# A cleared scratch tile between any two row gathers of a graph network kernel

## The chip, the cores and the metric

The kernel runs on one core of a Trainium2 chip. The metric is the device time of one execution in microseconds (us), the median of several runs. A core has TensorE (PE in the profile), VectorE (DVE), ScalarE (ACT), GpSimd (POOL) and SyncE (SP), each with a program of its own; they signal each other through semaphores. Sixteen DMA engines move data. An indirect DMA, which takes a list of row numbers, is issued by GpSimd, which is busy for a while with each.

## The reference, cut to what matters

Four graph layers run one after the other on 3125 nodes with 64 features and 50,000 edges. Each begins with a layer norm and a ReLU and adds its result to x. Three of them pass messages along edges:

```
# layer 0
msg  = relu(h[src] + edge_attr_16 @ We + be)
aggr = segment_sum(msg, dst)                  # then a two-layer MLP
# layer 2, three times
hx = h @ W_node[l]
a  = sigmoid(relu(concat(hx[dst], hx[src], edge_attr_3) @ Wa1 + ba1) @ Wa2 + ba2)
out = segment_sum(a * (hx[src] + ef), dst)    # ef: a small MLP of edge_attr_3
# layer 3
h = silu(bn(concat(x_i, x_j - x_i) @ W.T));  x_out = segment_sum(h, row)
```

Layer 1 is ten steps of a normalized propagation. It is done with dense blocks of the adjacency matrix, which are built during layer 0's pass, kept in HBM and streamed in; no row is gathered there.

## The kernel before, in words

The edges are first ordered by destination block and written to HBM by 400 scatters of GpSimd (line 755), as 416 tiles of 128 edges. Four tiles are a unit and eight units a body, so a message pass is 104 units in 13 bodies. There are five passes: one for layer 0, three for layer 2 and one for layer 3. The first is peeled, loops over the middle and peels the end on TensorE, VectorE and ScalarE; on SyncE and GpSimd all 13 bodies are one loop.

In a pass a unit goes through these hands:

- SyncE loads the edges' payload (`pay`, line 632) in four chunks of a body, two units each. It waits until those two units of the body before have been summed (`slots_free`).
- GpSimd (line 770) waits for the chunk, and then issues one gather per tile: eight per chunk, 32 per body, 416 per pass, 2080 in all. A gather brings 128 rows of the node table into `rows`, which has places for eight units. Its landing counts up `gathered[u]`.
- VectorE makes one-hot matrices of the destinations (lines 1102 and 1103), later adds the gathered rows to what TensorE worked out (lines 1115 to 1121), and in layer 0 it also makes the operands of the dense blocks (lines 1079, 1085 and 1087).
- ScalarE evicts and applies the activations: line 1466 (hidden layer) and 1468 in layer 2, 1489 and 1495 in layer 3.
- TensorE turns one-hots and payload (lines 1728 and 1605), multiplies (its matmuls all carry line 1502), and sums the messages of the unit before last into PSUM. The last matmul of that sum counts up `slots_free`.

The loop structure fixes the order on every engine; nothing is scheduled. GpSimd can be up to eight units ahead of the sum. Between passes 1 and 2, beside layer 1, GpSimd also issues 400 scatters of the second edge table (line 728); ahead of every eighth of them stand three small copies on GpSimd (lines 721, 719 and 724), the last of which the next scatters wait for.

`hold` (line 498) is a wait on a semaphore with an increment of a counter `held` that nobody waits for.

Of the kernel before, what the change touches and what calls it, by code (L numbers as in the profile page):

```python
# [34 lines left out]
K = 4  # L35
# [4 lines left out]
BODY = K * U  # L40
# [52 lines left out]
def gnn_kernel(nc, x, src, dst, edge_attr_16, edge_attr_3, edge_weight,  # L93
# [3 lines left out]
    with ExitStack() as ctx:  # L97
        def sb(name, shape, dt=F32):
            return ctx.enter_context(nc.sbuf_tensor(name, shape, dt))

        def sem(name):
            return ctx.enter_context(nc.semaphore(name))
# [20 lines left out]
        g_of = sb("g_of", [128, 1])  # L123
        ones_b = sb("ones_b", [128, EJ], BF16)
        zeros = sb("zeros", [128, CW])
        zeros_b = sb("zeros_b", [128, 512], BF16)
        acc_at = sb("acc_at", [1, 2, T], I32)
        tab_at = sb("tab_at", [1, 2, T], I32)
# [305 lines left out]
        hs_ready = sem("hs_ready")  # L434
        out_done = sem("out_done")
        held = sem("held")

        starts_ready = sem("starts_ready")
        starts_summed = sem("starts_summed")
# [56 lines left out]
        def hold(eng, semaphore, value):  # L496

            eng.wait_ge(semaphore, value)
            eng.sem_inc(held, 1)

        def load_values(eng, at_, lowest, highest):

            _, values = nc.values_load_multi_w_load_instructions(
                at_, engines=(eng.engine,), min_val=lowest, max_val=highest, skip_runtime_bounds_check_because=
                "the tables are worked out from counts of edges, and every entry is within its bounds by construction")
            return values
# [3 lines left out]
        def load_counts(eng, at_, lowest, highest):  # L510
            _, values = nc.values_load_multi_w_load_instructions(at_, engines=(eng.engine,), min_val=lowest, max_val=highest)
            return values
# [168 lines left out]
        def _(pool):  # L681
# [66 lines left out]
            def scatter_dst():  # L748

                for q in range(2 * G2):  # L750
                    h, j0 = q % 2, q * SG
                    pool.wait_ge(staged, q + 1)
                    pool.wait_ge(placed, next(c for c in range(NC_) if j0 + SG <= GR * (CHUNK_AT[c] + CHUNKS[c])) + 1)
                    for j in range(SG):
                        nc.gpsimd.indirect_dma_start(  # L755
                            rows_dst, bass.IndirectOffsetOnAxis(ap=pos_dst[:, j0 + j:j0 + j + 1], axis=0),
                            stage[:, h, j, :], None).then_inc(scattered[h], 16)

            def gather(ep, p, c_other, frm, width):
                hold(pool, table_in, 32 * (NP * ep + 1))  # L760
                with pool.Fori(0, NB) as i:
                    m = ep * NB + i
                    for c in range(CH):
# [3 lines left out]
                        for u in range(c * U // CH, (c + 1) * U // CH):  # L767
                            for k in range(K):
# [2 lines left out]
                                    rows[:, u, k, 0:width], None, frm,  # L771
                                    bass.IndirectOffsetOnAxis(ap=p[:, c, j, c_other:c_other + 1].bitcast(I32), axis=0)).then_inc(gathered[u], 16)

            pool.wait_ge(filled, 16 * 8)
            scatter_dst()
            gather(EP_L0, pay, C_OTHER, table, D)
# [1059 lines left out]
```

## Time and profile before

| | us |
|---|---|
| median of 3 runs | 4567.83 |
| lowest, highest | 4567.13, 4573.78 |
| profiled execution, its span | 5635.3 |
| GpSimd busy in it | 3082.6 |
| TensorE busy in it | 3433.8 |
| VectorE busy in it | 2812.2 |

The profile is that of one execution, and the time that it shows for it is its span; nothing is recorded around it. It is 1067.5 us longer than the median of the runs without a profile. Busy times leave out register, branch and semaphore instructions. "Remote" or "another core or an unknown queue" stands where the wait was ended by a semaphore event to which no instruction's end is close. On GpSimd the idle time "issue" is what lies between two instructions without any wait.

### The profile page before, as it was taken

The page shows a single profiled execution, that of the slowest core. Times are in us where ns is not written, and L with a number is a line of the kernel's source. Part 1 is how long each engine was busy: PE and PEld are TensorE (multiplying, and loading weights), DVE is VectorE, ACT ScalarE, POOL GpSimd, SP SyncE. Part 2 cuts the span into 40 slices and gives each one's busy share as a digit, 9 for nine tenths or more (in the row PEclk, how much of TensorE's full clock was granted, in tenths as well). Part 3 has the DMA queues.
Part 4 walks back from the last instruction along what each step waited for, and adds up shares of the span by engine and source line. Part 5 has one row for each costly group of instructions (what it writes and reads, how often), then busy time and mean ns, then how long its engine had stood idle before and what let it go on. Part 6 is the DMA issues. An engine that isn't in the chain of part 4 may idle for free.

```text
span 5635.3 us, 80038 instructions
## 1 busy us (share of the span) xinstructions
PE 3433.8 (61%) x20001; PEld 2425.2 (43%) x20012; DVE 2812.2 (50%) x10008; ACT 928.0 (16%) x3266; POOL 3082.6 (55%) x3058
## 2 busy tenths in 40 slices
PE   2440078878889999656656556666566666344444
PEld 2330034444433444355556455555455556233333
DVE  7840088878621111355555455555555556533333
ACT  0000023333200000011112111112111112111111
POOL 3787676656688880145555345555255554355544
PEclk9999999989899999777777577777677777555555
DMA  4311123323599999411111211112111112011101
GB/s 139 82 26 9 47 67 74 83 70 80 133 331 344 356 352 356 165 40 43 42 43 42 38 41 43 42 43 41 38 43 43 42 43 40 18 20 19 19 18 21
DMA packets 293594, 498.20 MB, mean 88 GB/s; under 512 B 169174, under 2 KB 207203, under 8 KB 291962
## 3 DMA queue, kind: packets, MB, share of 16 engines
q1 hardware_dynamic: 118407, 339.94, 17.0%
q0 software_dynamic: 92160, 115.72, 11.2%
q10 hardware_dynamic: 82800, 40.01, 2.5%
q8 instruction: 82, 1.34, 0.1%
q14 instruction: 145, 1.19, 0.1%
HBM read 435.57 MB, written 58.97 MB: 88 GB/s over the span
## 4 chain that ended last, share of the span: by engine, by line
PE 38%; another core or an unknown queue 21%; DVE 14%; issue 13%; POOL 8%; ACT 2%; DMA 1%; DVEq 1%; ACTq 1%; SPq 0%; POOLq 0%
PE ps L1502 34%; POOL rows_dst L755 8%; DVE arena L1103 3%; DVE arena L1102 2%; PE ps L1728 2%; DVE arena L1121 1%; DVE arena L1119 1%; PE ps L1605 1%; DVE arena L1117 1%; DMA arena<-in_edge_attr_dram 1%; PE ps L1680 1%; DVE arena L1275 1%; ACT arena L1468 1%; DVE arena L1280 1%
## 5 line engine op out<-in xcount | busy, mean ns | idle before, releaser
L770 POOL DMA_INDIRECT arena<-table,arena x2080 | 2085.0, 1002 | 2200.4 <-DMA arena<-rows_dst 1299.9
L1502 PE MATMUL ps<-arena 128*128 128x96 f32 (+3 forms) x9176 | 1605.9, 354 | 573.3 <-issue 174.3
L1502 PEld LDWEIGHTS ps<-arena 128*128 128x128 f32 (+3 forms) x9176 | 1138.9, 207 | 953.3 <-issue 623.6
L1605 PE MATMUL ps<-ident,arena 128*96 128x128 f32 x416 | 149.9, 360 | 1123.1 <-ACT arena L1468 570.6
L1102 DVE TENSOR_SCALAR arena<-iota_row_b,arena 128x128 bf16<-128x128 bf16 x1664 | 438.3, 264 | 695.4 <-remote 518.6
L1502 PE MATMUL ps<-arena,nodes 125*64 125x500 f32 (+2 forms) x3144 | 649.6, 538 | 27.2 <-DVEq L1194 16.5
L755 POOL DMA_INDIRECT rows_dst<-stage,arena x400 | 483.7, 1209 | 196.3 <-issue 121.6
L1103 DVE TENSOR_SCALAR arena<-iota_row_b,arena 128x128 f32<-128x128 bf16 x2080 | 582.5, 298 | 0.0
L1605 PEld LDWEIGHTS ps<-ident,arena 128*96 128x96 f32 x416 | 65.3, 157 | 1190.5 <-ACT arena L1468 588.3
L1115 DVE TENSOR_TENSOR arena<-ps,arena 128x256 f32<-128x256 f32 x416 | 175.4, 422 | 787.3 <-remote 614.9
L728 POOL DMA_INDIRECT rows_src<-stage,stage_at x400 | 485.1, 1213 | 118.5 <-issue 116.6
L1502 PEld LDWEIGHTS ps<-arena,nodes 125*64 125x64 f32 (+1 forms) x3144 | 241.4, 137 | 349.7 <-issue 317.8
L1728 PE MATMUL ps<-ident_b,arena 128*128 128x128 bf16 x1664 | 216.9, 271 | 225.1 <-DVE arena L1103 161.4
L1502 PE MATMUL ps<-we,arena 128*128 128x128 f32 x1248 | 336.0, 362 | 0.0
L1205 DVE TENSOR_TENSOR nodes<-nodes,ps 125x256 f32 (+1 forms) x70 | 27.5, 393 | 611.7 <-PE ps L1680 433.1
L1466 ACT ACTIVATE arena<-ps 128x256 f32<-128x256 f32 x312 | 119.7, 384 | 1257.9 <-remote 866.6
L1502 PE MATMUL ps<-wz,arena 96*128 96x128 f32 x1248 | 322.7, 352 | 0.0
L1502 PE MATMUL ps<-arena,wt 96*128 96x128 f32 x1248 | 271.7, 357 | 58.8 <-issue 31.8
L1728 PEld LDWEIGHTS ps<-ident_b,arena 128*128 128x128 bf16 x1664 | 148.3, 123 | 291.9 <-DVE arena L1103 199.2
L1502 PEld LDWEIGHTS ps<-we,arena 128*128 128x128 f32 x1248 | 271.2, 268 | 0.9
L1502 PEld LDWEIGHTS ps<-wz,arena 96*128 96x128 f32 x1248 | 269.3, 266 | 0.0
L1502 PEld LDWEIGHTS ps<-arena,wt 96*128 96x128 f32 x1248 | 236.0, 265 | 71.3 <-issue 37.0
(284 smaller groups left out, 3858.7 us busy)
## 6 DMA issues: line engine op xcount, KB each, us to landing
arena<-dense SPq DMA_DIRECT2D x240, 750.0 KB
nodes<-dense SPq DMA_DIRECT2D x60, 750.0 KB
dense<-arena ACTq DMA_DIRECT2D x150, 250.0 KB
arena<-table,arena POOLq DMA_INDIRECT x2080
arena<-dense SPq DMA_DIRECT2D x60, 500.0 KB
arena<-rows_dst SPq DMA_DIRECT2D x208, 96.0 KB
arena<-dense SPq DMA_DIRECT2D x6, 2000.0 KB
arena<-pair_rows SPq DMA_DIRECT2D x12, 976.6 KB
```

The source lines that it names most:

```text
L728: nc.gpsimd.indirect_dma_start(to, bass.IndirectOffsetOnAxis(ap=stage_at[:, h, j:j + 1], axis=0), stage[:, h, j, 0:width], None).then_inc( ...
L755: nc.gpsimd.indirect_dma_start(rows_dst, bass.IndirectOffsetOnAxis(ap=pos_dst[:, j0 + j:j0 + j + 1], axis=0), stage[:, h, j, :], None).the ...
L770: nc.gpsimd.indirect_dma_start(rows[:, u, k, 0:width], None, frm, bass.IndirectOffsetOnAxis(ap=p[:, c, j, c_other:c_other + 1].bitcast(I32 ...
L1102: nc.vector.tensor_scalar(of(ohb, v_)[:, k, :], iota_row_b[:], key_at, None, ALU.is_equal)
L1103: ins = nc.vector.tensor_scalar(of(oh, v_)[:, k, :], iota_row_b[:], key_at, None, ALU.is_equal)
L1115: nc.vector.tensor_tensor(sums, local_ps[:, :, :, 0], by_two(rows[:, v_ % U, :, at_:at_ + D]), ALU.add).then_inc(add_a, 1)
L1117: nc.vector.tensor_tensor(by_two(of(s1, v_)[:, 0]), edge_ps, by_two(rows[:, v_ % U, :, 0:D]), ALU.add)
L1119: nc.vector.tensor_tensor(sums, sums, local_ps[:, :, :, 1], ALU.add).then_inc(add_b, 1)
L1466: nc.scalar.activation(of(hid, v_), hid_ps, ACT.Relu).then_inc(hid_ready, 1)
L1502: return nc.tensor.matmul(to, lhsT, rhs, start=start, stop=stop, skip_group_check=True)
L1605: nc.tensor.transpose(to, pay[:, c, j:j + K, :].rearrange("p k c -> p (k c)"), ident[:]).then_inc(tr_ready, 1)
L1728: ins = nc.tensor.transpose(ohT_ps[:, k, :], of(ohb, v_)[:, k, :], ident_b[:])
```

## The change

GpSimd gets a tile `rest` of 128 x 100 32-bit floats, which nothing reads, and clears it after every gather. Each clear waits, on the semaphore `rested`, for the completion of the clear before it. The first finds the semaphore at one.

```
+        rest = sb("rest", [128, 100])
...
+        rested = sem("rested")
...
                                 nc.gpsimd.indirect_dma_start(
                                     rows[:, u, k, 0:width], None, frm,
                                     bass.IndirectOffsetOnAxis(...)).then_inc(gathered[u], 16)
 
+                                hold(pool, rested, m * BODY + (u * K + k + 1))
+                                nc.gpsimd.memset(rest[:], 0.0).then_inc(rested, 1)
+
+            pool.sem_inc(rested, 1)
             pool.wait_ge(filled, 16 * 8)
```

GpSimd's program before, at the first chunk of the first pass's loop (`arena` is `rows`, `table` the node table, and the waits of a row are in brackets):

```order
L761 UNCONDITIONAL_BRANCH [waits table_in]
L761 ISA
L498 ISA [waits pay_in0]
L770 DMA arena<-table,arena 128x64 [waits slots_free]
L770 DMA arena<-table,arena 128x64 x7
L498 REGISTER_ALU [waits pay_in1]
```

The same place now, up to the fourth gather (line numbers are two or three higher):

```order
L763 UNCONDITIONAL_BRANCH [waits table_in]
L763 ISA
L500 ISA [waits pay_in0]
L772 DMA arena<-table,arena 128x64 [waits slots_free]
L500 ISA
L777 MEMSET rest 128x100 [waits rested]
L772 DMA arena<-table,arena 128x64
L500 REGISTER_ALU
L777 MEMSET rest 128x100 [waits rested]
L772 DMA arena<-table,arena 128x64
L500 REGISTER_ALU
```

After each gather stand a register instruction and a clear that waits for the clear ahead of it; the next gather stands right behind it in the program. No other engine's program changes.

And the border between two chunks now:

```order
L777 MEMSET rest 128x100 [waits rested]
L500 REGISTER_ALU [waits pay_in1]
L772 DMA arena<-table,arena 128x64 [waits slots_free]
L500 REGISTER_ALU
L777 MEMSET rest 128x100 [waits rested]
```

A chunk's last clear comes ahead of the wait for the next chunk's payload.

## Rows read from the trace of the kernel before

**Rows 1.** The page, section 1: busy time, share, instructions.
```profile
PE 3433.8 (61%) x20001; PEld 2425.2 (43%) x20012; DVE 2812.2 (50%) x10008; ACT 928.0 (16%) x3266; POOL 3082.6 (55%) x3058
```

**Rows 2.** Windows, first to last gather of each pass (length, busy by engine, clock, DMA).
```profile
703.00:1490.00 787.00, 616.44 (x2928) 341.69 (x2929) 640.97 (x2379) 270.19 (x1409) 498.60 (x420) 0.92 0.34 74
2364.00:3120.00 756.00, 462.76 (x2922) 414.39 (x2922) 416.44 (x1518) 144.16 (x405) 398.09 (x416) 0.71 0.18 43
3187.00:3952.00 765.00, 451.32 (x2907) 405.02 (x2907) 419.56 (x1517) 144.00 (x405) 398.07 (x416) 0.72 0.18 42
4019.00:4778.00 759.00, 462.44 (x2922) 414.64 (x2922) 418.96 (x1519) 144.72 (x405) 397.10 (x416) 0.72 0.18 42
4852.00:5600.00 748.00, 325.31 (x1576) 253.49 (x1576) 278.55 (x1101) 96.69 (x200) 394.23 (x416) 0.50 0.12 19
```

**Rows 3.** Timeline of GpSimd, two chunks in layer 2's pass (start, length, instruction, idle before).
```profile
2938.92 0.94 POOL L770 DMA_INDIRECT arena<-table,arena  x1 [0.30 <-issue]
2940.17 0.95 POOL L770 DMA_INDIRECT arena<-table,arena  x1 [0.30 <-issue]
2941.42 0.94 POOL L770 DMA_INDIRECT arena<-table,arena  x1 [0.30 <-issue]
2947.08 0.94 POOL L770 DMA_INDIRECT arena<-table,arena  x1 [4.72 <-DMA arena<-rows_dst]
```

**Rows 4.** Timeline of ScalarE over the same stretch, line 1466.
```profile
2933.82 0.38 ACT L1466 ACTIVATE arena<-ps 128x256 f32<-128x256 f32 x1 [2.99 <-PE ps L1502]
2943.96 0.38 ACT L1466 ACTIVATE arena<-ps 128x256 f32<-128x256 f32 x1 [7.85 <-remote]
2948.51 0.38 ACT L1466 ACTIVATE arena<-ps 128x256 f32<-128x256 f32 x1 [2.84 <-PE ps L1502]
```

**Rows 5.** Timeline of TensorE in layer 3's pass.
```profile
5229.65 0.61 PE L1728 MATMUL ps<-ident_b,arena 128*128 128x128 bf16 x4 [1.87 <-issue]
5230.34 2.02 PE L1502 MATMUL ps<-arena 128*128 128x96 f32 x8
5243.62 0.82 PE L1502 MATMUL ps<-arena 125*128 x4 [11.26 <-ACT arena L1489]
```

**Rows 6.** Timeline of ScalarE in the same stretch of layer 3's pass.
```profile
5242.89 0.58 ACT L1489 COPY arena<-ps 128x512 bf16<-128x512 bf16 x1 [16.92 <-remote]
5245.92 0.58 ACT L1489 COPY arena<-ps 128x512 bf16<-128x512 bf16 x1 [2.12 <-PE ps L1728]
5250.24 0.58 ACT L1489 COPY arena<-ps 128x512 bf16<-128x512 bf16 x1 [3.33 <-PE ps L1728]
```

**Rows 7.** The chain that ended last, by engine.
```profile
PE 38%; another core or an unknown queue 21%; DVE 14%; issue 13%; POOL 8%; ACT 2%; DMA 1%; DVEq 1%; ACTq 1%; SPq 0%; POOLq 0%
```

**Rows 8.** Waits, whole span (who, for what: us in total, times, longest).
```profile
ACT arena L1466 <- remote: 866.6, 132, 28.7
POOL arena L770 <- issue: 595.9, 1871, 1.7
POOL rows_src L728 <- POOL stage_at L724: 0.7, 4, 0.2
```

**Rows 9.** Timeline of GpSimd where copies stand between two scatters.
```profile
2008.38 1.19 POOL L728 DMA_INDIRECT rows_src<-stage,stage_at  x1 [0.30 <-issue]
2009.88 1.18 POOL L728 DMA_INDIRECT rows_src<-stage,stage_at  x1 [0.30 <-issue]
2011.32 0.19 POOL L724 COPY stage_at<-pos_src 125x8 int32 x1
2011.68 1.21 POOL L728 DMA_INDIRECT rows_src<-stage,stage_at  x1 [0.18 <-issue]
```

**Rows 10.** Groups of GpSimd by line and shape: its clears (busy, mean ns).
```profile
L706 POOL MEMSET arena<- 128x104 f32 x1 | 0.3, 291 | 0.0
L700 POOL MEMSET we<- 128x128 f32 x1 | 0.2, 206 | 0.0
```

**Rows 11.** Line 770 in layer 0's pass (duration ns min/median/max).
```profile
L770 POOL DMA_INDIRECT arena<-table,arena x416: 938/1090/2384, 703.0 to 1487.0; - x139
```

## The prediction

> **What bounds the kernel now.** I read the page's busy shares first. No engine is full: TensorE is busy for 61% of the span, GpSimd for 55%, VectorE for 50% [rows 1]. Then the windows of the five message passes, where all that changes lies [rows 2]. From first to last gather they last 787, 756, 765, 759 and 748 us. In the last four GpSimd is busy for only 394 to 398 us, TensorE for 325 to 463, VectorE for 279 to 420. Something holds all of them.
>
> The timelines show what. GpSimd issues gathers at a pitch of 1.25 us: 0.94 busy and 0.30 of issue [rows 3]. Eight make a chunk, and then it waits 4.72 us for the next payload. So two units take 8 x 1.25 + 4.72 - 0.30 = 14.4 us. ScalarE takes one unit 4.55 us after the other, but needs 10.14 us for the one before, and spends 7.85 of these in a wait for "remote" [rows 4]. In layer 3 the same is plainer: TensorE ends its transposes at 5230.26, yet ScalarE's copy, which needs nothing else, starts at 5242.89, and TensorE waits 11.26 us for it [rows 5, 6]. Signals between engines arrive late while GpSimd streams gathers, and the chain gives 21% of the span to that unknown [rows 7]; on one ScalarE line alone these waits are 866.6 us [rows 8].
>
> Now the point on which everything hangs. The profiled span is 5635.3 us and the median of the runs 4567.8: 1067.5 us are not there without the profile. 21% of the span is 1183 us. Is the late signal a thing of the profiled execution? I test it by a sum. Undisturbed, a unit takes 4.32 us in layer 3 (5245.92 to 5250.24) [rows 6] and 4.55 in layer 2 [rows 4], while GpSimd needs 4 x 1.25 = 5.0 for its gathers. So without late signals a pass of layers 2 and 3 runs at GpSimd's pace, 416 x 1.25 = 520 us, with some ten us for loop ends 530. The four take 3028 now, so 908 would go. In layer 0 VectorE is busy for 641 of 787 us [rows 2]; at most 146 would go. 5635 - 908 - 146 = 4581, and the median is 4568. Had the other engines' own pace set these passes, it would be 312 x 4.55 + 104 x 4.32 = 1869 for the four passes, and 4330 in all, 238 too little. So I take it that the runs outside the profile are free of late signals, and that **GpSimd's pitch of gathers bounds four of the five passes**. That is an inference from a sum, and it is what a rival denies.
>
> **The change part by part.** It adds 2080 clears of 128 x 100 floats, one behind each gather, 2080 register instructions and 2080 waits, all on GpSimd. It removes nothing and moves nothing on another engine.
>
> *The clear itself.* Clears of nearly this size took 0.206 us (128 x 128) and 0.291 (128 x 104, with gaps between its elements) [rows 10]. Ours is contiguous; I take 0.19, a little under the 128 x 128 one. What it adds to the pitch is less than that, since part of the 0.30 us of issue between two indirect DMAs passes beside it. Between two scatters with three copies the pitch was 2011.68 - 2009.88 = 1.80 us against 2009.88 - 2008.38 = 1.50 without [rows 9]: 0.30 for three. A copy begins without a gap as the scatter ends (2009.88 + 1.18 = 2011.06, and the third began at 2011.32), and after the last the gap is 0.18 instead of 0.30. With one clear the pitch becomes 0.94 + 0.19 + 0.18 = 1.31 us, so 0.06 more. Bounds: 0 if it fits wholly into the issue gap; with a clear of 0.29 and the full 0.30 behind it, 0.29 more.
>
> *The wait.* A clear waits for the clear before it. Between them stands a gather of 0.94 us, and the next gather is already in the program ahead of the next wait, so the signal has nearly a microsecond to arrive. Where a scatter waited for GpSimd's own copy it cost 0.7 us in 4 times, 0.18 each [rows 8], far less. Queued behind a late clear are the next gathers, and for them VectorE waits. I cost the wait at nothing, 0.18 if the cover is gone. The 2080 register instructions run ahead on the queue beside a gather; nothing too.
>
> *VectorE beside it.* In layer 0, where VectorE is dense, a gather's median is 1.09 us against a best of 0.938 [rows 11]; in the later passes it is 398 / 416 = 0.957 on average [rows 2]. The clear goes the same way to SBUF, so I add 0.02 us in the later passes and 0.05 in layer 0, for the clear or for the VectorE instruction that it holds up. The Trainium skill (SBUF - State Buffer, Who interferes with whom) says that GpSimd shares a port pair with VectorE's 2-port modes, and that whichever comes second blocks fully. The longer gathers of layer 0 agree with it. By that rule a clear that comes first makes a VectorE instruction wait for all its 0.19 us; were it so each time in layer 0, where VectorE nearly bounds, the sum would be 58 us higher.
>
> *The sum.* Later passes: 1664 x (0.06 + 0.02) = 133 us, all on the path if GpSimd bounds them. Layer 0: 416 x (0.06 + 0.05) = 46 us; VectorE is the nearer bound there (641 us busy against 416 x 1.25 to 1.4 = 520 to 580 for GpSimd), so I count about half, 24. Together 157. In the profiled execution's own time that is 5635 + 157 = 5792, as far as its late signals stay as they are. The pass there too is a run of gathers and a wait behind it, so that a longer run lengthens it. Since the added instructions are on GpSimd alone, I carry the 157 us unchanged to the runs: 4568 + 157 = **4725 us**. The bounds 0 and 0.29 us per gather give 4568 and about 5150.
>
> **The rivals.**
>
> *A. Late signals are real in every execution, and the clears break them up: faster.* For it: the stalls are large and lie in streams of gathers: the copy of layer 2 that came 7.85 us late fell behind the last gather of its run, at 2942.36 [rows 3, 4]. The clear waits for GpSimd's own signal, so if signals are late the stream pauses by itself until they come. Place: all five passes. The point from which it decides is how far a pass without a profile exceeds 416 x 1.31 = 545 us, the floor with clears. Against it: if the rest of the program (5635 - 3028 - 787 = 1820 us) is as long without the profile and layer 0 takes 641 to 787, the four passes take 1961 to 2107 together, 490 to 527 each, already under that floor. Only if the rest were some 150 us shorter would they be at about 565, with 20 each to gain: 4568 - 80 = 4490. Chance 16%.
>
> *B. The wait on its own signal is not covered: much slower.* Each clear, and with it the gather behind, starts only after the signal of the clear before and a fresh issue: 0.18 + 0.18 us on top of the 0.06. 2080 x 0.36 = 749 more on the longest view, some 4568 + 157 + 500 = 5200 where layer 0 hides its part and chunks end with idle time. For it: nothing in the trace shows GpSimd waiting for its own clears. Against: the gather of 0.94 us between. Chance 12%.
>
> *C. No change within the measurement.* GpSimd has slack of its own in the runs without a profile, or the clear fits in the issue gap of 0.30 us. For it: GpSimd's idle waits for payload, 4.72 us in each 14.4 [rows 3], are many times 8 x 0.08 us. Against: those waits came behind late signals. The time would be 4568. Chance 12%.
>
> *Forecast,* 60%: 4725, with a range of its own of 4620 to 4860.
>
> **How the numbers follow.** A measurement of this kernel can tell about 0.2%, 9 us, from no change. Faster is nearly all of A and a little of the others: 0.17. Same is C with its edges taken off: 0.11. Slower is the forecast and B: 0.72. The range of 8 in 10 goes down to 4530, which leaves out about half of A and a bit, and up to 4980, which leaves out the upper part of B: 4530 to 4980.
>
> **What would show it.** In the changed kernel's profile the clear should stand right behind each gather with 0.17 to 0.22 us, and a gather 0.18 us behind it, pitch 1.31 (in layer 0 up to 1.5). The line of the clears should have no waits for GpSimd's own signal beyond 0.1 us. The profiled span itself may well move the other way than the median, if late signals are broken up there: shorter "remote" waits on ScalarE with a slower median would be the forecast's mechanism and not a contradiction. The forecast is wrong if the pitch rises by over 0.3 us (B), if it rises and the median stays (C: GpSimd does not bound), or if the median falls, which would show that the late signals belong to the runs too.

## The result

The changed kernel takes 4707.52 us (median of 4 runs, 4705.4 to 4709.95) against 4567.68 (4 runs, 4567.13 to 4573.78): a ratio of 1.0302, 95% interval 1.0289 to 1.0315, so 140 us slower. The forecast was 4725 us.

Its profiled execution has a span of 4705.7 us, and no late signals. From section 1 of its page, which answers to [rows 1]:

```profile
PE 3255.5 (69%) x20011; PEld 2215.8 (47%) x20012; DVE 2788.7 (59%) x10008; ACT 933.7 (20%) x3266; POOL 3530.2 (75%) x5138
```

GpSimd has 2080 more instructions and is busy for 448 us more than in [rows 1], and for 429 us more than in the undisturbed profile of the kernel before, `again` below (3101.2 us). The chain of the same page, which answers to [rows 7], now leads through GpSimd and no longer through an unknown queue:

```profile
POOL 34%; issue 31%; PE 24%; DVE 5%; DMA 2%; DVEq 1%; POOLq 1%; ACT 1%; SPq 1%; ACTq 0%
```

A comparison with the profile ahead of the prediction would mislead, for that execution was disturbed. So the kernel before was profiled again (the run `again` below); its span is 4562.8 us. The windows from first to last gather of its five passes (columns as in [rows 2]):

```profile
702.00:1397.00 695.00, 578.72 (x2955) 332.77 (x2956) 637.78 (x2395) 273.23 (x1422) 522.06 (x416) 0.98 0.39 84
2256.00:2779.00 523.00, 419.28 (x2973) 347.39 (x2973) 422.69 (x1548) 147.85 (x414) 396.01 (x416) 0.92 0.25 61
2841.00:3365.00 524.00, 416.87 (x2975) 344.64 (x2975) 423.29 (x1548) 148.42 (x415) 396.77 (x416) 0.93 0.25 61
3427.00:3950.00 523.00, 416.15 (x2969) 344.78 (x2970) 422.78 (x1548) 147.72 (x413) 396.24 (x416) 0.92 0.26 61
4020.00:4541.00 521.00, 350.99 (x1636) 258.79 (x1636) 288.81 (x1141) 104.74 (x207) 394.29 (x416) 0.50 0.17 28
```

And those of the changed kernel:

```profile
702.00:1404.00 702.00, 582.45 (x2957) 336.15 (x2958) 638.98 (x2399) 273.25 (x1422) 602.40 (x834) 0.97 0.40 84
2261.00:2818.00 557.00, 428.23 (x2973) 360.00 (x2974) 421.76 (x1548) 147.50 (x414) 483.06 (x832) 0.89 0.25 57
2881.00:3440.00 559.00, 428.71 (x2976) 360.19 (x2976) 420.39 (x1548) 148.38 (x415) 483.94 (x832) 0.89 0.24 57
3502.00:4059.00 557.00, 432.80 (x2974) 367.47 (x2975) 421.29 (x1548) 147.19 (x415) 483.23 (x832) 0.88 0.25 57
4129.00:4684.00 555.00, 351.11 (x1636) 258.64 (x1636) 287.65 (x1141) 104.75 (x207) 480.27 (x831) 0.50 0.17 26
```

The reader sees where the 140 us are: each of the four later passes has grown by 34 to 36 us (523, 524, 523, 521 to 557, 559, 557, 555; to a tenth of a us, 2089.5 to 2227.9, so 138.4 together), and layer 0's pass by 6 or 7 (695.4 to 701.7). VectorE and ScalarE do the same work in the same time, only with more idle time between. TensorE is busy for 9 to 17 us longer in each of the passes of layer 2, at a granted clock of 0.88 to 0.89 instead of 0.92 to 0.93.

In the timeline of GpSimd in the first pass of layer 2, the kernel before (`again`):

```profile
2600.94 0.94 POOL L770 DMA_INDIRECT arena<-table,arena  x1 [0.30 <-issue]
2602.18 0.95 POOL L770 DMA_INDIRECT arena<-table,arena  x1 [0.30 <-issue]
```

and the changed one:

```profile
2599.82 0.95 POOL L772 DMA_INDIRECT arena<-table,arena  x1 [0.17 <-POOL rest L777]
2600.77 0.20 POOL L777 MEMSET rest<- 128x100 f32 x1
2601.13 0.95 POOL L772 DMA_INDIRECT arena<-table,arena  x1 [0.16 <-POOL rest L777]
```

The pitch is 1.31 us instead of 1.25: 0.95 of gather, 0.20 of clear, 0.16 of gap. In the kernel before, GpSimd has next to no idle time beyond the issue gap within a later pass; it is the bound. The group of the clears in the changed kernel's whole trace (busy, mean ns of one, idle time before them):

```profile
L777 POOL MEMSET rest<- 128x100 f32 x2080 | 458.3, 220 | 1.0
```

The clears start right behind their gathers: the engine was idle for 1.0 us ahead of all 2080 together. So no clear waited noticeably for the signal of the clear before.

Not in the forecast is this place, a pause of 1.67 us that no wait explains:

```profile
2410.41 0.95 POOL L772 DMA_INDIRECT arena<-table,arena  x1 [0.16 <-POOL rest L777]
2411.35 0.20 POOL L777 MEMSET rest<- 128x100 f32 x1
2413.22 1.17 POOL L772 DMA_INDIRECT arena<-table,arena  x1 [1.67 <-issue]
```

In the four later passes 18 gathers start 2.8 to 2.9 us after the one before. The first stands behind the 113th gather of these passes, and each next one 88 gathers further on. In `again` no distance inside a pass is like that; there are three of 2.0 to 2.9 us at the first gathers of a pass, which the changed kernel has too.

The disturbed profile of the kernel before, which has no clears, shows the same pause. Behind the same 113th gather:

```profile
2568.28 0.94 POOL L770 DMA_INDIRECT arena<-table,arena  x1 [4.82 <-DMA arena<-rows_dst]
2570.90 1.05 POOL L770 DMA_INDIRECT arena<-table,arena  x1 [1.67 <-issue]
2572.25 0.94 POOL L770 DMA_INDIRECT arena<-table,arena  x1 [0.30 <-issue]
```

It stands there at 16 of the 18 places, 2.61 us from start to start each time, and at each of the 16 GpSimd had waited 4 us or more for payload just one gather earlier. Behind the other such waits inside these passes there is no pause. At the two places where it had not waited (behind the 9th and the 361st gather of layer 3's pass) the distance is the usual 1.25 us. So the pause does not come from the clears. It goes by the number of gathers and not by that of instructions, since the changed kernel has more instructions for each gather and pauses at the same places. Loading of instructions does not fit either: from 2400 to 2780 us of the changed kernel's trace, where four of the pauses lie, the trace has no packet of an instruction queue.

### The profile page after: what moved, and what is told of

It reads as the page before. It is cut to its first block, busy times and chain, and to the rows that moved or that the text cites. A ratio compares the mean times of both kernels' runs of the same rounds, so it can differ in the third digit from the quotient of the medians.

```text
span 4705.7 us, 86289 instructions
## 1 busy us (share of the span) xinstructions
PE 3255.5 (69%) x20011; PEld 2215.8 (47%) x20012; DVE 2788.7 (59%) x10008; ACT 933.7 (20%) x3266; POOL 3530.2 (75%) x5138
## 4 chain that ended last, share of the span: by engine, by line
POOL 34%; issue 31%; PE 24%; DVE 5%; DMA 2%; DVEq 1%; POOLq 1%; ACT 1%; SPq 1%; ACTq 0%
PE ps L1508 23%; POOL arena L772 16%; POOL rows_dst L757 10%; POOL rest L777 8%; PE ps L1686 1%; DVE arena L1091 1%; DMA arena<-in_edge_attr_dram 1%; DMA arena<-table,arena 1%; DVE arena L1093 1%; POOLq L501 1%; DVEq L505 1%; PE ps L1648 1%; DVE arena L1085 0%; DMA arena<-rows_dst 0%; DVE arena L1109 0%
## 5 line engine op out<-in xcount | busy, mean ns | idle before, releaser
L1508 PE MATMUL ps<-arena 128*128 128x96 f32 (+3 forms) x9176 | 1485.0, 339 | 714.4 <-DVE arena L1127 378.4
L1508 PEld LDWEIGHTS ps<-arena 128*128 128x128 f32 (+3 forms) x9176 | 1036.0, 198 | 1125.1 <-issue 748.0
L1108 DVE TENSOR_SCALAR arena<-iota_row_b,arena 128x128 bf16<-128x128 bf16 x1664 | 472.1, 286 | 1.9 <-PE ps L1508 1.0
L777 POOL MEMSET rest<- 128x100 f32 x2080 | 458.3, 220 | 1.0
L1611 PE MATMUL ps<-ident,arena 128*96 128x128 f32 x416 | 124.6, 300 | 372.4 <-DMA arena<-rows_dst 279.0
L1508 PE MATMUL ps<-we,arena 128*128 128x128 f32 x1248 | 295.4, 324 | 0.0
L1508 PE MATMUL ps<-wz,arena 96*128 96x128 f32 x1248 | 286.3, 317 | 0.0
L1391 ACT ACTIVATE arena<-ps 128x125 f32<-128x125 f32 x625 | 163.7, 276 | 481.6 <-PE ps L1508 447.8
L1481 ACT ACTIVATE arena<-arena,ba2c 128x4 f32<-128x4 f32 x312 | 92.8, 297 | 812.5 <-DVE arena L1286 780.7
L1508 PEld LDWEIGHTS ps<-wz,arena 96*128 96x128 f32 x1248 | 232.9, 232 | 0.0
L1091 DVE TENSOR_SCALAR arena<-iota_row_b,arena 128x128 bf16<-128x128 bf16 x858 | 232.5, 336 | 0.3 <-issue 0.2
```

Of the source, the lines that this page charges most:

```text
L777: nc.gpsimd.memset(rest[:], 0.0).then_inc(rested, 1)
L1091: nc.vector.tensor_scalar(lhs[:, slot, part, :], iota_row_b[:], lo_col[:, bass.ds(tile_at, 1)], w_left[:, part, bass.ds(tile_at, 1)], ALU. ...
L1108: nc.vector.tensor_scalar(of(ohb, v_)[:, k, :], iota_row_b[:], key_at, None, ALU.is_equal)
L1391: ins = nc.scalar.activation(ev[:, slot, r * LO:(r + 1) * LO], ps[:, bank, r * LO:(r + 1) * LO], ACT.Copy, accum_out=deg_parts[:, bass.ds( ...
L1508: return nc.tensor.matmul(to, lhsT, rhs, start=start, stop=stop, skip_group_check=True)
L1611: nc.tensor.transpose(to, pay[:, c, j:j + K, :].rearrange("p k c -> p (k c)"), ident[:]).then_inc(tr_ready, 1)
```

## The experiments

The questions: is it GpSimd's pitch that bounds, what in the added instructions costs, and what were the late signals. All ratios are to the kernel before, run on the same chip.

**again: the kernel before, once more.**

> The kernel before, unchanged, profiled once more. If late signals are a regular thing of its profiled execution, the span is again near 5635 us with waits for 'remote' of some 7 to 12 us in each stream of gathers. If they were an accident of one execution, the span is near 4570 and the passes of layers 2 and 3 last about 530 us each (416 x 1.25 = 520 and loop ends), with GpSimd almost never idle in them.

Measured: 4564.6 us in one execution, with a span of 4562.8. The late signals belong to that one profiled execution: in each of the thirteen other profiles the waits for "remote" add up to 16 us or less, none of them in a stream of gathers. ScalarE's line 1466, whose waits for "remote" were 866.6 us [rows 8], waits for 328.7 us in this one, all of it for TensorE.

**waitonly: the wait without the clear.**

```
                                 hold(pool, rested, m * BODY + (u * K + k + 1))
-                                nc.gpsimd.memset(rest[:], 0.0).then_inc(rested, 1)
+                                pool.sem_inc(rested, 1)
```

> Wait and increment of 'rested' after each gather, without a clear. Theory P: nothing runs on GpSimd's cores between two gathers, the pitch stays 1.25, 4568 within 10 us. Theory W: the wait costs, 4650 to 4710. For the profile: if the wait alone is what keeps signals from coming late, its span is near the time of the runs; if the clear is needed, the span is again near 5600.

Measured: 4564.58 us, ratio 0.9999 (0.9990 to 1.0009). Waits, increments and register instructions alone cost nothing. GpSimd's program makes the increment itself here, so this run says nothing of a wait for an instruction of the engine to end. What the run was to tell of late signals it could not, as they did not recur.

**unit: one clear per unit.**

```
+                                if k == K - 1:
+                                    hold(pool, rested, m * U + (u + 1))
+                                    nc.gpsimd.memset(rest[:], 0.0).then_inc(rested, 1)
```

> One clear of 128 x 100 per unit, behind each fourth gather, instead of four. Theory P: a quarter of the cost, 4568 + 140 / 4 = 4603. Theory W gives the same quarter, so this run is for the late signals: with a break behind every fourth gather the profiled span is near 4605 if any break suffices, and over 5000 if each gather needs one.

Measured: 4590.83 us, ratio 1.0055 (1.0040 to 1.0070), 25 us and not 35. Each later pass grew by 6.5 us (523 to 529 or 530), 0.062 us for each of its 104 clears: the pitch term alone. At the 18 places of the pauses this trace shows nothing over 1.3 us.

**col1: a clear of one column.**

```
-        rest = sb("rest", [128, 100])
+        rest = sb("rest", [128, 1])
```

> The clear is of 128 x 1 instead of 128 x 100, with the wait as it was. Theory P (GpSimd's pitch of gathers bounds the later passes; what counts is clear plus 0.18 us of gap against the bare gap of 0.30): a clear of about 0.1 us gives a pitch of 0.94 + 0.10 + 0.18 = 1.22, so 0.03 under the bare 1.25 and about 1664 x 0.03 = 50 us faster than the kernel before, some 4520. Theory W (it is the wait on GpSimd's own signal and the extra instructions that cost, not the clear's width): still 4700 to 4710. In between, with a pitch of exactly 1.25: 4568.

Measured: 4597.29 us, ratio 1.0063 (1.0049 to 1.0077). I had expected a gain of 50 us and got a loss of 30. From the timeline of GpSimd:

```profile
2603.65 0.94 POOL L772 DMA_INDIRECT arena<-table,arena  x1 [0.19 <-POOL rest L777]
2604.59 0.11 POOL L777 MEMSET rest<- 128x1 f32 x1
2604.90 0.94 POOL L772 DMA_INDIRECT arena<-table,arena  x1 [0.19 <-POOL rest L777]
```

The pitch is 1.25, as without a clear, and the gap has grown from 0.16 to 0.19 to make it so. So 1.25 us is a floor of the pitch of these gathers; what keeps it was not found. The 30 us are elsewhere: the pauses stand in this trace too, at the same 18 places. Distances over 1.9 us exceed the pitch by 31.3 us in all, against 3.6 in `again`.

**later and l0only: clears in some passes only.**

```
+                                if ep != EP_L0:      # later
+                                    hold(pool, rested, (m - NB) * BODY + (u * K + k + 1))
...
+                                if ep == EP_L0:      # l0only
+                                    hold(pool, rested, m * BODY + (u * K + k + 1))
```

> Clears only in the four passes of layers 2 and 3, none in layer 0's. Theory P (GpSimd's pitch is what those four passes cost, and layer 0's is bound elsewhere): about 134 of the 140 us remain, since layer 0's pass grew by only 6.3 us in the profile (695.4 to 701.7): 4700 us. A rival: the clears hold VectorE up in layer 0 and that is worth the 24 us that the prediction gave it: 4683.

Measured: 4703.67 us, ratio 1.0289 (1.0275 to 1.0303), 132 us slower.

> Clears only in layer 0's pass. The counterpart of the run with clears in the later passes alone, which left 134 of the 140 us: 4 to 6 us here, 4573. The prediction had 24: 4592.

Measured: 4569.91 us, ratio 1.0001 (0.9992 to 1.0010). Layer 0's 416 clears are worth between nothing and 5 us. The later passes carry the loss. The 6.3 us by which layer 0's pass had grown between two profiles show nothing: without any clear in it that pass lasts 695.4 us in `again`, 696.0 in waitonly, 703.6 in later and 707.4 in pe_more.

**ring2: two scratch tiles in turn.**

```
-        rest = sb("rest", [128, 100])
+        rest = sb("rest", [128, 2, 100])
...
-                                nc.gpsimd.memset(rest[:], 0.0).then_inc(rested, 1)
+                                nc.gpsimd.memset(rest[:, k % 2], 0.0).then_inc(rested, 1)
...
-            pool.sem_inc(rested, 1)
+            pool.sem_inc(rested, 2)
```

> Two scratch tiles in turn, so that a clear waits for the clear before the last instead of the last. Theory P (the wait is covered): the same as the changed kernel, 4707 within 10 us. Rival (some of the cost is the wait on GpSimd's own signal): faster by up to 100 us.

Measured: 4684.9 us, ratio 1.0247 (1.0231 to 1.0263), 0.55% under the changed kernel's ratio: some 25 us. My expectation was wrong. What ended GpSimd's idle time ahead of the gathers of the later passes, in the changed kernel:

```profile
  POOL rest L777: 266.0, 1642
...
  issue: 30.1, 18
```

and in ring2:

```profile
  POOL rest L777: 267.0, 1638
...
  issue: 3.5, 22
```

The gap behind the clears is the same. Gone are 26.6 us of "issue", the 18 pauses (the 22 waits left in ring2 are short). A small rest of them is left in ring2 at each of the 18 places, 1.39 to 1.61 us from start to start instead of 1.31. Behind the 113th gather:

```profile
2414.28 0.95 POOL L772 DMA_INDIRECT arena<-table,arena  x1 [0.16 <-issue]
2415.24 0.20 POOL L777 MEMSET rest<- 128x100 f32 x1
2415.78 0.95 POOL L772 DMA_INDIRECT arena<-table,arena  x1 [0.35 <-POOL rest L777]
```

So the tight wait did cost, though its signal was prompt. The reading that fits all the traces is this: the pause is in GpSimd's program, in the kernel before too, and stays hidden as long as the program has run ahead of the engine. A wait for payload uses that lead up (the profile of the kernel before), and so does a wait for the clear just before (the changed kernel); a wait one clear further back leaves most of it. That the program runs ahead is inferred from this pattern; the profile does not show it directly.

**col1ring2: both.** One column, two tiles.

> Clears of 128 x 1 on two scratch tiles in turn. Theory S: the 30 us of col1 are pauses of GpSimd's instruction stream of about 1.5 us behind each 88th gather (20 of them in the four later passes of its profile), which are covered when a clear may wait for the clear before the last: 4568 within 10 us, and no distance between gathers over 2.5 us inside these passes. Rival: the 30 us are the clears' own cost, spread over all gathers: 4597 as before.

Measured: 4576.05 us, ratio 1.0017 (1.0008 to 1.0026). Of col1's 29 us some 21 are gone (1.0063 to 1.0017), and of the distances over 2.5 us one is left in the later passes, at a pass's first gathers. Some 8 us are left (4 to 12 by the interval). Rests of the pauses are about 5 of them: at the 18 places the distance is 1.52 to 1.64 us instead of 1.25. The others stay unaccounted for. The expectation spoke of 20 pauses in the later passes of col1; there are 18.

**col40 and col200: other widths.** 40 and 200 columns in place of 100.

> A clear of 128 x 40. By the model (pitch = the larger of 1.249 and 0.95 + clear + 0.16, clear = 0.12 + 0.0008 per column) the clear takes 0.15 and the pitch is 1.26: 1664 x 0.01 = 17 us on top of the 30 of col1, so 4615. If cost were in proportion to columns from 1 up (no floor), the value lies at 4597 + 0.4 x 110 = 4641.

Measured: 4612.74 us, ratio 1.0102 (1.0087 to 1.0118). The pitch is 1.259, as the model had it.

> A clear of 128 x 200. The model is pitch = the larger of 1.249 and 0.95 + clear + 0.16, from col1 (1.249 with a clear of 0.12) and the changed kernel (1.311 with 0.20). A clear of 200 columns should take about 0.29 (0.12 for 1, 0.20 for 100), so the pitch is 1.39 to 1.40 and the four passes are 1664 x 0.085 = 140 us longer than with 100 columns; 4850. If layer 0's pass begins to feel it too, up to 4890. If VectorE or TensorE bound and the clear only disturbs them, well under 4800.

Measured: 4877.74 us, ratio 1.0674 (1.0658 to 1.0690). GpSimd's timeline:

```profile
2600.38 0.28 POOL L777 MEMSET rest<- 128x200 f32 x1
2600.83 0.95 POOL L772 DMA_INDIRECT arena<-table,arena  x1 [0.17 <-POOL rest L777]
2601.78 0.28 POOL L777 MEMSET rest<- 128x200 f32 x1
2602.22 1.13 POOL L772 DMA_INDIRECT arena<-table,arena  x1 [0.16 <-POOL rest L777]
2603.35 0.39 POOL L777 MEMSET rest<- 128x200 f32 x1
2603.90 0.95 POOL L772 DMA_INDIRECT arena<-table,arena  x1 [0.16 <-POOL rest L777]
```

The median pitch is 1.397 us, 0.086 more than with 100 columns: 143 us over 1664 gathers. The later passes together are 177 us longer than with 100 columns (2227.9 to 2404.4). The rest is in rows like those at 2602.22 and 2603.35: a gather of 1.13 us instead of 0.95, a clear of 0.39 instead of 0.28. Distances over the median by 0.03 or more (pauses left out) add up to 7 us in `again`, 19 with 100 columns and 55 with 200. The long clears show who is in the way. In the later passes 131 clears of the changed kernel took over 0.24 us and 227 clears of col200 over 0.32; every one of them began while VectorE ran the instruction that makes a one-hot matrix in bf16 (line 1108, in the kernel before 1102), and no clear that began elsewhere took so long. The Trainium skill's rule of the shared port pair (SBUF - State Buffer, Who interferes with whom) agrees with this in kind. What lengthened the gathers was not looked for.

**pe_more: more work on TensorE.**

```
+                        mm(hid_ps[:, 0, :], wt[:, 0, :], of(payT, v_))
                         for q in range(K // 2):
                             ins = mm(hid_ps[:, q, :], wt[:, q, :], of(payT, v_))
```

> The kernel before, with one of layer 2's two hidden-layer matmuls of each unit done twice (same result): about 0.3 us more on TensorE per unit, 312 units. Theory P: TensorE has slack beside GpSimd's 5.0 us per unit, so the time stays 4567 within 10 us. Rival T (TensorE's path sets the pace of a unit): 312 x 0.3 = 90 us slower, about 4660.

Measured: 4569.84 us, ratio 1.0001 (0.9991 to 1.0010). The added matmuls are there (623 of the kind in the first pass's window, 416 in `again`). But TensorE's busy time in it rose only from 419 to 427 us and not by the 31 intended, since its granted clock rose from 0.92 to 0.96. Three passes with 8 us each would be 24 us, and the interval ends at some 5. So TensorE is not on the path of layer 2's passes, though the test was weaker than meant.

**three: a quarter of the gathers less.** In the later passes the fourth gather of each unit is left out, and VectorE waits for three.

```
-                            for k in range(K):
+                            for k in range(K if ep == EP_L0 else K - 1):
...
-                v.wait_ge(gathered[v_ % U], 16 * K * (m + 1))
+                v.wait_ge(gathered[v_ % U], 16 * (K - 1) * (m + 1) + 16 * NB)
```

> The kernel before with every fourth gather of the four passes of layers 2 and 3 left out, so that a quarter of the messages of these layers are made from stale rows; all else is done. It tells where the next bound lies. GpSimd then needs 3 x 1.249 = 3.75 us per unit. Theory P: the passes fall to the other engines' pace, which the first profile gave as 4.55 us (layer 2) and 4.32 (layer 3) per unit: 4568 - 312 x 0.45 - 104 x 0.68 = 4357 us. If GpSimd bounded even then: 4568 - 416 x 1.25 = 4050. If it never bounded: 4568.

Measured: 4193.98 us, ratio 0.9175 (0.9161 to 0.9190), 376 us faster. I had said 211. The window of the first pass of layer 2 in it:

```profile
2262.00:2690.00 428.00, 377.61 (x2972) 312.75 (x2972) 416.88 (x1550) 147.28 (x415) 300.19 (x312) 0.99 0.26 59
```

GpSimd is now busy for 300 of 428 us and VectorE for 417. VectorE's share makes it the likely next bound there, at 4.1 us per unit; no run slowed VectorE alone to show it. ScalarE's line 1466 shows the pace of units:

```profile
2404.73 0.38 ACT L1466 ACTIVATE arena<-ps 128x256 f32<-128x256 f32 x1 [1.10 <-PE ps L1502]
...
2408.64 0.38 ACT L1466 ACTIVATE arena<-ps 128x256 f32<-128x256 f32 x1 [1.10 <-PE ps L1502]
...
2412.55 0.38 ACT L1466 ACTIVATE arena<-ps 128x256 f32<-128x256 f32 x1 [0.93 <-PE ps L1502]
...
2416.78 0.38 ACT L1466 ACTIVATE arena<-ps 128x256 f32<-128x256 f32 x1 [1.10 <-PE ps L1502]
```

So the pace of 4.55 us that the prediction read for an undisturbed unit of layer 2 was too slow by half a microsecond. TensorE's granted clock was 0.71 in that window [rows 2], between its two levels of 1.2 and 2.4 GHz, and is 0.99 here; how much of the difference the clock makes was not tested. For layer 3 the pace of 4.32 us was right. Its pass in this run:

```profile
3721.00:4169.00 448.00, 325.32 (x1600) 258.89 (x1600) 282.30 (x1123) 99.34 (x204) 297.35 (x312) 0.50 0.15 25
```

That is 4.3 us per unit, at a granted clock of 0.50, the lower level, as in the disturbed profile and in `again`; neither GpSimd nor VectorE is full there. Layer 3's pass became 74 us shorter (71 expected), and layer 2's three some 306 (140 expected).

No run of the twelve beats the kernel before with all of its work done.

## Why the prediction was right, point by point

*Late signals are not in the runs, and GpSimd's pitch bounds the later passes: right.* The sum put the disturbance-free kernel at 4581 us; the profile taken again is at 4563. It put a later pass at 530 us; they are 521 to 523. More work on TensorE costs nothing (pe_more), taking gathers away gains 376 us (three). The bound on the other engines' own pace, 4.55 us per unit of layer 2, was misread (three); it was far enough below GpSimd's 5.0 us for the argument to hold either way. Rival A falls: no signals were late, and nothing was to be gained.

*A clear of 0.19 us adds 0.06 to the pitch: right.* It takes 0.20, and the medians of the pitch are 1.249 and 1.311: 0.062 x 1664 = 103 us, where the prediction had 100. The working behind it was right by luck in one place: it read the gap of 0.18 behind a copy as a cost by itself, and by that a narrow clear should have gained. There is a floor at 1.25 (col1).

*VectorE in the way, 0.02 us in the later passes, 33 us: too much.* The longer distances grew by 12 us with 100 columns. With 200 they grew by 48, so the term is real and not in proportion. The long clears all began beside one kind of VectorE instruction (col200).

*The wait costs nothing: wrong, by some 25 us.* This is the step that failed. The prediction looked at whether the signal comes in time, and it does (1.0 us of idle time ahead of all 2080 clears). It did not ask whether the wait would uncover something else: 18 pauses of GpSimd's program. They stood in the very profile that it read, as distances of 2.61 us behind a wait for payload. With the wait one clear back it is 25 us less (ring2). Rival B had the place right, but its price of 500 us and its mechanism, a signal that comes late, wrong.

*Layer 0, 24 us: too much.* It is 0 to 5 (l0only). VectorE is busy for 638 of 695 us there, and its busy time did not grow (639).

Against the two profiles, 4562.8 and 4705.7, the later passes come to 103 (pitch) + 27 (pauses and first gathers, 30.3 against 3.6) + 12 (longer distances) = 142 us, where their lengths give 138. The 4 us between them are distances a little under the median.

That 157 came within 17 us of the measured 140 is partly luck. The terms for VectorE (21) and for layer 0 (some 20) were too large, and the terms for the wait (27) and the pitch (3) too small; errors of 41 and 30 us largely cancelled. A pass's idle wait for payload in the first profile [rows 3], on which rival C stood, is not there in an undisturbed one.

## What to carry to other kernels

Where an engine issues a stream of indirect DMAs at a steady pitch and is never idle otherwise, what is put between two of them is paid as far as it does not fit into the gap of that pitch (here a clear of 0.20 us cost 0.06, and one of 0.11 nothing), though the engine's busy share is only half or three quarters. When a profile's span lies well over the runs' median, test with a sum whether the excess and a suspicious wait are the same thing, and take another engine's pace from it only where the granted clock is that of an undisturbed stretch; a second profile settles it. And a wait that is always met in time can still cost, by using up the lead that hid pauses of the engine's own program. Look for such pauses where the stream has just stood still.

## What was not expected of the hardware

- Signals between engines came 7 to 13 us late in the stretches read of one of fourteen profiled executions, whose span was 1073 us longer than that of the next one of the same kernel (5635.3 and 4562.8). The cause is open.
- An indirect DMA of 128 rows keeps GpSimd busy for 0.94 us, but in a stream they came every 1.25 us and no closer, even when a clear of 0.11 us stood between. What sets this pitch is open.
- GpSimd's program pauses for some 1.6 us every 88 gathers, with clears and without. The pause shows where a clear that waits for the clear before follows every gather, and in the kernel before where the stream had just waited for payload. With a wait one clear further back at most 0.4 us of it shows, and with one clear for four gathers nothing. What the pause is stays open.
